# A state-space block and a routed expert layer: start, tail, router's choice and the table of stages rewritten

## The chip, the cores and the metric

One NeuronCore of a Trainium2 chip runs the whole program. Its engines work side by side and meet through semaphores: TensorE (PE), VectorE (DVE), ScalarE (ACT), GpSimd (POOL) and SyncE (SP), which issues most transfers (DMA). The metric is the device time of one execution in microseconds (us), lower is better. Three runs of the kernel before gave 2983.3, 2983.3 and 2991.5, median 2983.32. A difference of 0.3% or more (9 us) is counted as one.

## What is computed

Sixteen rows of 512 tokens by 256 features, all fp32. Two halves, each modulated by its own vectors (scale, shift, gate) made from a condition `c`:

```
mod = (silu(c) @ wmod).reshape(16, 6, 1, 256)          # sa, ca, ga, sb, cb, gb
h = layernorm(x) * (1 + ca) + sa
x = x + ga * mamba(h)                                  # norm, W_in, conv of 3, W_dt, scan over 512 steps
h = layernorm(x) * (1 + cb) + sb
x = x + gb * moe(h)                                    # 16 experts, all computed, weighted by the router
# scan: h = exp(dt * A) * h + (dt * x) * B ;  y = sum over 16 states of h * C
# router: scores = sigmoid(h @ gate.T); choice = scores + e_bias; 4 groups of 4 experts
#   group score = sum of its two best; keep 2 groups; in them the 4 best experts; weights normalised
```

The scan runs over 512 inner channels by 16 states. The experts are computed densely (every token through all 16) and combined with the router's weights, which are zero for those not chosen.

## The kernel before, in words

**Slots.** Each of the 16 rows has a slot of 32 units (`NU`). A unit is one state `n` of one pair of channel tiles: ScalarE makes the decays (`decay`, L981, two exponentials), GpSimd the drive (`drive`, L1120), VectorE scans 1024 elements (`scan`, L714) and multiplies by C (`times_c`, L721), and GpSimd adds the product to `gsum`, by its own adds for four units of sixteen and by an accumulating transfer (L1143) for the rest. SyncE broadcasts B and C rows from DRAM for each unit.

**The table.** A unit has 3 moments, a slot 96. All other work of the neighbouring rows is cut into steps and set beside the scan by the table in `streams`: an entry `(name, row, steps, first, final)` spreads the steps of a stage over the moments from first to final. The row before (`behind`) runs `mix1`, `project`, `stats` (second layernorm), `turn` (transposes, router logits), `pick` (router's choice, VectorE), `weigh` (weights transposed and stored); the row after (`coming`) runs `load_x`, `norms`, `turn_in`, `silu_first`/`silu_last` (convolution), `rows_bc`, `step_sizes0`; the slot's own row `gates`, `mix0`, `step_sizes1`. The experts of the row behind run from moment 35 of its slot to moment 22 of the next (`EXPERTS_AT`). Each engine has its own instruction order made by the same table, with a lag in moments: PE 0, ACT 1, DVE 2, POOL and SP 3. No engine reorders: what stands behind a waiting instruction waits too.

**Start.** SyncE issues all weights; then the modulation is computed and stored to DRAM; then 12 chunks of expert weights (512 KB each, three buffers in `gsum`) are loaded, transposed by PE through the three `wbank` buffers, and copied out half by ScalarE (L999), half by VectorE (L770); only then are the stages of row 0 done (`first_row`), and the first scan starts.

**Tail.** After the last scan the experts of row 14 finish over `TAIL` units, then `last_row` runs the stages of row 15 alone, then its 17 expert steps. A step is the gate and up products of one pair of experts on half the tokens (L461), tanh (L971), two products (L686, L693), the weighting (L1108) and the down product of the step before (L473).

**The choice.** `pick` has three parts (`yield` between them) and 22 waits and counts of its own semaphore, `ROUTE_V` = 26 per row.

## Time and profile before

| | us |
|---|---|
| median of three runs | 2983.32 |
| profiled execution | 2979.56 |
| its span, first to last instruction | 2977.7 |
| start, to the first scan | 131.31 |
| slot 0 | 140.09 |
| slot 1 | 164.68 |
| slots 2 to 14, each | 171 to 174 |
| slot 15 | 156.3 |
| tail, from the last scan's end | 147.9 |

VectorE is busy for 84% of the span, PE 81%, GpSimd 75%, ScalarE 53%; the mean granted clock of PE is 0.913. A slot is counted from its first scan to the next slot's. The idle time of an engine in front of an instruction stands in brackets with what released it, and a wait matters for the time only where the waiting engine is one that the others wait for.

### The profile page before, as it was taken

How to read it: one execution, taken by the hardware profiler on the slowest of the kernel's cores; microseconds unless marked ns; L12 is line 12 of the kernel's file. 1: busy time of each engine (PE TensorE's matmuls, PEld its weight loads, DVE VectorE, ACT ScalarE, POOL GpSimd, SP SyncE). 2: the span in 40 equal slices, each digit the busy share in tenths (PEclk: the TensorE clock that was granted, in tenths of full speed). 3: DMA queues.
4: the chain of work that ended last, by engine and by line, in shares of the span. 5: the costliest groups of instructions: out<-in, count | busy, mean ns of one | idle time of the engine just before them, and what ended most of it. 6: DMA issues, size and time to landing. Idle time of an engine off the chain costs nothing.

```text
span 2977.7 us, 29259 instructions
## 1 busy us (share of the span) xinstructions
PE 2415.1 (81%) x9004; PEld 1705.8 (57%) x9004; DVE 2495.4 (84%) x2673; ACT 1574.1 (53%) x2945; POOL 2234.5 (75%) x1514
## 2 busy tenths in 40 slices
PE   3525697988979798888979898897979889797879
PEld 2212465666746566665656566565656657565668
DVE  1389898989889898998989899898989889898932
ACT  2556555555556555555655555565565556554311
POOL 0388887878887787887878788787877878887912
PEclk8767898989989898998999899898999999898989
DMA  5188887787888777888887788788877878887921
GB/s 155 51 217 215 217 211 194 207 220 194 216 216 224 194 201 209 208 210 213 223 205 199 208 206 209 205 215 217 204 204 197 212 198 219 217 206 193 241 56 50
DMA packets 337374, 584.76 MB, mean 196 GB/s; under 512 B 50224, under 2 KB 153136, under 8 KB 337216
## 3 DMA queue, kind: packets, MB, share of 16 engines
q1 hardware_dynamic: 281920, 381.54, 41.1%
q0 software_dynamic: 55296, 201.35, 35.1%
q8 instruction: 71, 1.16, 0.2%
q14 instruction: 87, 0.71, 0.1%
HBM read 371.38 MB, written 10.06 MB: 128 GB/s over the span
## 4 chain that ended last, share of the span: by engine, by line
PE 39%; POOL 23%; issue 12%; DMA 10%; DVE 9%; ACT 6%; SPq 1%; POOLq 0%; DVEq 0%; ACTq 0%
PE wbank L461 12%; DMA gsum<-unit 9%; POOL unit L1120 9%; PE mbank L473 6%; POOL gsum L1143 4%; PE wbank L379 4%; DVE hbank L714 4%; PE wbank L417 3%; PE wbank L489 3%; POOL act L1108 3%; PE wbank L367 2%; PE wbank L437 2%; PE wbank L403 2%; POOL rstd L1043 2%; DVE unit L721 1%
## 5 line engine op out<-in xcount | busy, mean ns | idle before, releaser
L1120 POOL TENSOR_TENSOR unit<-dtx,b_bc 128x1024 f32<-128x1024 f32 x512 | 1310.5, 2578 | 11.0 <-DMA b_bc<-bc_scratch 9.2
L714 DVE TENSOR_TENSOR_SCAN hbank<-hbank,unit 128x1024 f32<-128x1024 f32 x512 | 1172.8, 2291 | 26.2 <-ACT hbank L981 20.9
L981 ACT ACTIVATE hbank<-dt,a_neg 128x512 f32<-128x512 f32 x1024 | 668.8, 680 | 319.6 <-DVE unit L721 316.8
L721 DVE TENSOR_TENSOR unit<-hbank,c_bc 128x1024 f32<-128x1024 f32 x512 | 624.1, 1219 | 28.8 <-DVE hbank L714 0.9
L1108 POOL TENSOR_TENSOR act<-act,w_all 128x512 f32<-128x512 f32 x256 | 356.8, 1394 | 299.0 <-DVE act L693 298.6
L473 PE MATMUL mbank<-down_t,act 128*128 128x256 f32 x2048 | 501.8, 382 | 55.1 <-POOL act L1108 52.3
L461 PE MATMUL wbank<-h_t,up_t 128*128 128x256 f32 x2048 | 490.0, 382 | 38.9 <-DVE xb L560 24.9
L461 PE MATMUL wbank<-h_t,gate_t 128*128 128x256 f32 x2048 | 502.9, 390 | 21.7 <-DVE act L686 14.4
L1143 POOL DMA_DIRECT2D gsum<-unit x384 | 366.2, 954 | 150.4 <-DVE unit L721 92.9
L473 PEld LDWEIGHTS mbank<-down_t,act 128*128 128x128 f32 x2048 | 382.8, 190 | 156.9 <-POOL act L1108 74.9
L461 PEld LDWEIGHTS wbank<-h_t,gate_t 128*128 128x128 f32 x2048 | 397.0, 196 | 125.8 <-DVE act L686 27.9
L461 PEld LDWEIGHTS wbank<-h_t,up_t 128*128 128x128 f32 x2048 | 384.9, 190 | 136.4 <-DVE xb L560 42.1
L971 ACT ACTIVATE etanh<-wbank 128x512 f32<-128x512 f32 x256 | 151.0, 590 | 401.2 <-PE wbank L461 401.2
L686 DVE SCALAR_TENSOR_TENSOR act<-etanh,wbank 128x512 f32<-128x512 f32 x256 | 173.9, 679 | 127.4 <-ACT etanh L971 127.3
L379 PE MATMUL wbank<-xb,w_dt 128*128 128x512 f32 x512 | 231.4, 596 | 8.6 <-DVE xb L560 8.4
L403 PE MATMUL wbank<-xn_t,w_in 128*128 128x512 f32 x256 | 182.1, 864 | 66.8 <-DVE gz L577 56.6
L351 PE MATMUL wbank<-ident,z 128*128 128x128 f32 x256 | 52.2, 359 | 173.5 <-ACT z L822 173.5
L693 DVE TENSOR_TENSOR act<-act,wbank 128x512 f32<-128x512 f32 x256 | 173.8, 679 | 18.5 <-PE wbank L461 13.6
L489 PE MATMUL wbank<-gsum,ident 128*128 128x512 f32 x256 | 130.3, 621 | 65.9 <-DMA gsum<-unit 65.9
L1037 POOL TENSOR_SCALAR nmean<-sums 128x4 f32<-128x4 f32 x48 | 20.5, 427 | 193.3 <-ACT ht L809 173.0
L379 PEld LDWEIGHTS wbank<-xb,w_dt 128*128 128x128 f32 x512 | 97.6, 191 | 110.5 <-issue 106.5
L1136 POOL TENSOR_TENSOR gsum<-unit 128x1024 f32<-128x1024 f32 x64 | 155.2, 2424 | 1.4 <-DVE unit L721 1.4
(124 smaller groups left out, 2534.0 us busy)
## 6 DMA issues: line engine op xcount, KB each, us to landing
gsum<-unit POOLq DMA_DIRECT2D x384, 512.0 KB, 7.5
b_bc<-bc_scratch SPq DMA_DIRECT2D x512, 256.0 KB, 6.4
c_bc<-bc_scratch SPq DMA_DIRECT2D x512, 256.0 KB, 5.7
w_all<-w_scratch SPq DMA_DIRECT2D x256, 256.0 KB, 4.4
ht<-in_L_attn_x_dram SPq DMA_DIRECT2D x16, 512.0 KB, 9.2
xt<-in_L_attn_x_dram SPq DMA_DIRECT2D x16, 512.0 KB, 9.0
out_dram<-xt SPq DMA_DIRECT2D x16, 512.0 KB, 3.3
z<-mod_scratch SPq DMA_DIRECT2D x16, 256.0 KB, 8.6
```

Source lines behind the costliest of these rows:

```text
L379: m = eng.matmul(t.bank[:, :], w_dt[:, k, m_ * P:(m_ + 1) * P], xb[:, xb_at(row, k), :], start=k == 0, stop=k == DK - 1)
L403: m = eng.matmul(t.bank[:, :], w_in[:, k, (DK + q) * P:(DK + q + 1) * P], xn_t[:, k, :], start=k == 0, stop=k == HK - 1)
L461: m = eng.matmul(t.bank[:, j * HT:(j + 1) * HT], w[:, 2 * first + j, k, :], h2_t[:, row % 2, k, h * HT:(h + 1) * HT], start=k == 0, stop=k ...
L473: m = eng.matmul(mbank[:, u * H:(u + 1) * H], act[:, (n - 1) % MOE_RING, j, u * P:(u + 1) * P], down_t[:, e, :], start=(e == 0 and u == 0) ...
L489: m = eng.matmul(t.bank[:, :], ident[:, :], gsum[:, (2 * p + k) % SUMS, a, :], start=False, stop=k == 1)
L686: eng.scalar_tensor_tensor(out=a, in0=etanh[:, :], scalar=1.0, in1=t.bank[:, :], op0=ALU.add, op1=ALU.mult).then_inc(t.free, 1)
L714: eng.tensor_tensor_scan(h, h, unit[:, g % RING, :, :].rearrange("p a t -> p (a t)"), 0.0, ALU.mult, ALU.add).then_inc(scanned, 1)
L721: eng.tensor_tensor(unit[:, g % RING, :, :], hbank[g % HB][:, :, :], c_bc[:, s:s + 1, :].to_broadcast([P, 2, T]), ALU.mult).then_inc(c_sca ...
L981: eng.activation(hbank[g % HB][:, a, :], dt[:, 2 * q + a, :], ACT.Exp, scale=a_neg[:, 2 * q + a, n:n + 1]).then_inc(decayed, 1)
L1108: eng.tensor_tensor(a, a, w_all[:, n % W_RING, :, :], ALU.mult).then_inc(weighted, 1)
L1120: eng.tensor_tensor(unit[:, g % RING, :, :], dtx[:, 2 * q:2 * q + 2, :], b_bc[:, s:s + 1, :].to_broadcast([P, 2, T]), ALU.mult).then_inc(d ...
L1143: eng.dma_start(o, unit[:, g % RING, :, :], accum_op=ALU.add).then_inc(summed[k], 16)
```

## The change

Four parts.

*Start.* SyncE loads what the modulation needs first, then row 0 of x, then the other weights and three chunks. ScalarE does the first layernorm of row 0 ahead of everything else, then the modulation. Only 4 of the 12 chunks (`EARLY`) are turned before the first scan; the other 8 are turned in slot 0, at moments 4 to 40. Their buffers are now both halves of `xt` and `act`.

*Choice.* `pick` computes a group's score as the greatest sum of two of its members, counts better groups with a small negative margin in place of greater-or-equal-and-earlier, and fuses scaling, masks and weights into `scalar_tensor_tensor` operations; `ROUTE_V` becomes 16.

*Table.* Many entries are moved by some moments, `gates` from 24..42 to 29..35 and `weigh` from 28..34 to 33..35 the most; `load_res` and `load_gb` come later; the lag of SP becomes 2.

*Tail.* `last_streams` sets the stages of row 15 among the last experts of row 14. Row 15's experts follow.

ScalarE at the program's start, before (then after). L986/L1006 is the exponential of `A_log`, L987/L998 and L993/L1004 the modulation, L999/L989 the copies of turned chunks, L809, L817, L822 (L808, L816, L821) sums, squares and scaling of a layernorm:

```order
L986 ACT_TABLE_LOAD
L986 ACTIVATE a_neg<-a_neg 128x64
L987 ACTIVATE dtx<-dtx 128x32
L993 ACTIVATE gz<-dt 16x256 x2
L999 ACTIVATE gate_t<-wbank 128x512
...
L999 ACTIVATE down_t<-wbank 128x512
L809 ACTIVATE ht,sums<-ht 128x256 x4
L817 ACTIVATE z,squares<-ht,nmean 128x256 x4
L822 ACTIVATE ht<-ht,shift,rstd 128x256 x4
L809 ACTIVATE ht,sums<-ht 128x256 x4
```

```order
L808 ACT_TABLE_LOAD
L808 ACTIVATE ht,sums<-ht 128x256 x4
L816 ACTIVATE z,squares<-ht,nmean 128x256 x4
L821 ACTIVATE ht<-ht,shift,rstd 128x256 x4
L998 ACTIVATE dtx<-dtx 128x32
L1004 ACTIVATE gz<-dt 16x256 x2
L1006 ACTIVATE a_neg<-a_neg 128x64
L989 ACTIVATE gate_t<-wbank 128x512
L989 ACTIVATE up_t<-wbank 128x512
L989 ACTIVATE down_t<-wbank 128x512
L989 ACTIVATE gate_t<-wbank 128x512
L808 ACTIVATE ht,sums<-ht 128x256 x4
```

The first layernorm stands ahead of the modulation now, and four copies are left between them and the second layernorm, where twelve were.

PE in slot 1, between the transposes of the second layernorm (L351, L352) and the first experts (L461, L476), before (then after). `w_in` are the gates of the slot's row, `w_tok` the router's weights:

```order
L351 MATMUL wbank<-ident,z 128x128 x8
L437 MATMUL wbank<-router_t,h_t 128x16 x8
L403 MATMUL wbank<-xn_t,w_in 128x512 x4
L351 MATMUL wbank<-ident,w_tok 16x128 x4
L403 MATMUL wbank<-xn_t,w_in 128x512 x2
L461 MATMUL wbank<-h_t,gate_t 128x256 x4
L461 MATMUL wbank<-h_t,up_t 128x256 x4
L403 MATMUL wbank<-xn_t,w_in 128x512 x2
```

```order
L352 MATMUL wbank<-ident,z 128x128 x8
L438 MATMUL wbank<-router_t,h_t 128x16 x8
L404 MATMUL wbank<-xn_t,w_in 128x512 x6
L352 MATMUL wbank<-ident,w_tok 16x128 x4
L404 MATMUL wbank<-xn_t,w_in 128x512 x2
L476 MATMUL wbank<-h_t,gate_t 128x256 x4
L476 MATMUL wbank<-h_t,up_t 128x256 x4
```

Three of four gates now stand ahead of the weights, the fourth right behind them, and all ahead of the experts.

PE in the tail, before: the last experts of row 14 (L461, L473), then `mix1` (L486, L489), `project` (L417, L419), `turn`, `weigh`, and row 15's first expert:

```order
L461 MATMUL wbank<-h_t,gate_t 128x256 x4
L461 MATMUL wbank<-h_t,up_t 128x256 x4
L473 MATMUL mbank<-down_t,act 128x256 x8
L486 MATMUL wbank<-xb,diag_d 128x512
L489 MATMUL wbank<-gsum,ident 128x512 x2
L486 MATMUL wbank<-xb,diag_d 128x512
L489 MATMUL wbank<-gsum,ident 128x512 x2
L417 MATMUL wbank<-w_out,gz 128x256 x4
...
L351 MATMUL wbank<-ident,z 128x128 x8
L437 MATMUL wbank<-router_t,h_t 128x16 x8
L351 MATMUL wbank<-ident,w_tok 16x128 x4
L461 MATMUL wbank<-h_t,gate_t 128x256 x4
```

The same place after, in two pieces, up to the first expert of row 15:

```order
L476 MATMUL wbank<-h_t,up_t 128x256 x4
L501 MATMUL wbank<-xb,diag_d 128x512
L504 MATMUL wbank<-gsum,ident 128x512 x2
L501 MATMUL wbank<-xb,diag_d 128x512
L504 MATMUL wbank<-gsum,ident 128x512 x2
L488 MATMUL mbank<-down_t,act 128x256 x2
L418 MATMUL wbank<-w_out,gz 128x256 x4
```

```order
L488 MATMUL mbank<-down_t,act 128x256 x2
L476 MATMUL wbank<-h_t,gate_t 128x256 x4
L476 MATMUL wbank<-h_t,up_t 128x256 x4
L488 MATMUL mbank<-down_t,act 128x256 x2
L352 MATMUL wbank<-ident,z 128x128 x8
L488 MATMUL mbank<-down_t,act 128x256 x2
L438 MATMUL wbank<-router_t,h_t 128x16 x8
L476 MATMUL wbank<-h_t,gate_t 128x256 x4
L476 MATMUL wbank<-h_t,up_t 128x256 x4
L488 MATMUL mbank<-down_t,act 128x256 x2
L352 MATMUL wbank<-ident,w_tok 16x128 x4
L488 MATMUL mbank<-down_t,act 128x256 x6
```

Two expert steps of row 14 now stand between `project` and the weights. The diff, cut to its core:

```diff
     EXPERTS_AT = (35, 118)
     EP = E // 2
+    LAST_EXPERTS_AT = (31, 122)
     HALVES = 4 * (E + 1)
-    ACT_LAG, DVE_LAG, POOL_LAG, SP_LAG = 1, 2, 3, 3
+    EARLY = 4
+    ACT_LAG, DVE_LAG, POOL_LAG, SP_LAG = 1, 2, 3, 2
     TAIL = 9
...
             behind, coming = slot - 1, slot + 1
-            plan = []
+            plan = [] if slot else [("chunks", 0, 2 * (len(chunks) - EARLY), 4, 40)]
             if behind >= 0:
-                plan += [("mix1", behind, 4, 6, 7), ("load_res", behind, 1, 1, 2), ("load_gb", behind, 1, 6, 30),
+                plan += [("mix1", behind, 4, 6, 7), ("load_res", behind, 1, 11, 11), ("load_gb", behind, 1, 57, 61),
                          ("project", behind, 4, 16, 16), ("stats", behind, 5, 19, 21),
-                         ("turn", behind, 4, 24, 25), ("pick", behind, 5, 26, 28), ("weigh", behind, 2, 28, 34)]
-            plan += [("step_sizes1", slot, 9, 1, 7), ("load_ga", slot, 1, 53, 60), ("gates", slot, 9, 24, 42),
-                     ("mix0", slot, 4, 51, 64)]
+                         ("turn", behind, 4, 24, 24), ("pick", behind, 5, 26, 28), ("weigh", behind, 2, 33, 35)]
+            plan += [("step_sizes1", slot, 9, 1, 7), ("load_ga", slot, 1, 57, 59), ("gates", slot, 9, 29, 35),
+                     ("mix0", slot, 4, 51, 63)]
             if coming < NB:
-                plan += [("load_x", coming, 1, 20, 24), ("norms", coming, 12, 25, 39), ("turn_in", coming, 2, 42, 47),
-                         ("silu_first", coming, 6, 56, 59), ("silu_last", coming, 6, 63, 65),
-                         ("rows_bc", coming, 3, 77, 84),
+                plan += [("load_x", coming, 1, 19, 26), ("norms", coming, 12, 25, 39), ("turn_in", coming, 2, 44, 47),
+                         ("silu_first", coming, 6, 56, 59), ("silu_last", coming, 6, 61, 65),
+                         ("rows_bc", coming, 3, 78, 83),
                          ("step_sizes0", coming, 9, 73, 79)]
             return [Steps(stage[name](row), n, first, final) for name, row, n, first, final in plan if name in stage]
...
-                        pass
+        def last_streams(stage):
+
+            last = NB - 1
+            plan = [("load_res", last, 1, 9, 12), ("mix1", last, 4, 5, 5), ("project", last, 4, 7, 7),
+                    ("stats", last, 5, 5, 9), ("turn", last, 4, 11, 12), ("load_gb", last, 1, 23, 23),
+                    ("pick", last, 5, 11, 15), ("weigh", last, 2, 13, 20)]
+            return [Steps(stage[name](row), n, first, final) for name, row, n, first, final in plan if name in stage]
...
+                tanhs = t.bank[:, 0:TT * E].rearrange("p (t e) -> p t e", e=E)
+                bias = choice_bias[:, :].rearrange("p (a e) -> p a e", a=1).to_broadcast([P, TT, E])
                 need.wait_ge(route_act, row + 1)
-                eng.tensor_scalar(scores, scores, 0.5, 0.5, ALU.mult, ALU.add).then_inc(route_v, 1)
+                eng.scalar_tensor_tensor(out=r_ch[:, :, :], in0=tanhs, scalar=0.5, in1=bias, op0=ALU.mult,
+                                         op1=ALU.add).then_inc(route_v, 1)
+                eng.tensor_scalar(r_s[:, :, :], tanhs, 1.0, None, ALU.add).then_inc(t.free, 1)
+                members = r_ch[:, :, :].rearrange("p t (g m) -> p (t g) m", m=GRP)
                 need.wait_ge(route_v, at + 1)
-                eng.tensor_copy(r_s[:, :, :], scores).then_inc(route_v, 1)
-                eng.tensor_tensor(r_ch[:, :, :], scores, bias, ALU.add).then_inc(route_v, 1)
-                eng.tensor_tensor(scores, scores, bias, ALU.add).then_inc(route_v, 1)
-                choice = scores.rearrange("p t (g m) -> p t g m", m=GRP)
-                pairs = r_ch[:, :, :].rearrange("p t (g m) -> p (t g) m", m=GRP)
-                kept = r_ch[:, :, :].rearrange("p t (g m) -> p t g m", m=GRP)
-                hi, lo = (r[:, :, :].rearrange("p (t g) m -> p t g m", t=TT) for r in (r_hi, r_lo))
+                eng.tensor_tensor(r_two[:, :, 0:3], members[:, :, 0:3], members[:, :, 1:4], ALU.add).then_inc(route_v, 1)
+                eng.tensor_tensor(r_two[:, :, 3:5], members[:, :, 0:2], members[:, :, 2:4], ALU.add).then_inc(route_v, 1)
+                eng.tensor_tensor(r_two[:, :, 5:6], members[:, :, 0:1], members[:, :, 3:4], ALU.add).then_inc(route_v, 1)
                 need.wait_ge(route_v, at + 4)
...
+                eng.tensor_reduce(r_g[:, :], r_two[:, :, :], AX.X, ALU.max).then_inc(route_v, 1)
...
+                need.wait_ge(route_v, at + 5)
+                eng.tensor_tensor(r_gt[:, :, :, :], other, this, ALU.subtract).then_inc(route_v, 1)
+                need.wait_ge(route_v, at + 6)
+                eng.tensor_tensor(r_gt[:, :, :, :], r_gt[:, :, :, :], low, ALU.is_gt).then_inc(route_v, 1)
+                need.wait_ge(route_v, at + 7)
...
+                need.wait_ge(route_v, at + 8)
+                eng.scalar_tensor_tensor(
+                    out=r_tmp[:, :, 0:E].rearrange("p t (g m) -> p t g m", m=GRP),
+                    in0=r_cnt[:, :].rearrange("p (t g a) -> p t g a", t=TT, a=1).to_broadcast([P, TT, NGRP, GRP]),
+                    scalar=1.5, in1=members.rearrange("p (t g) m -> p t g m", t=TT), op0=ALU.is_lt,
+                    op1=ALU.mult).then_inc(route_v, 1)
+                yield
...
+                need.wait_ge(t.free, t.after)
+                need.wait_ge(route_v, at + 12)
+                eng.scalar_tensor_tensor(out=r_w[:, :, 0:E], in0=r_cut[:, :, 0:E], scalar=TAKEN, in1=r_s[:, :, :],
+                                         op0=ALU.is_equal, op1=ALU.mult).then_inc(route_v, 1)
+                need.wait_ge(route_v, at + 13)
                 eng.tensor_reduce(r_den[:, :], r_w[:, :, :], AX.X, ALU.add).then_inc(route_v, 1)
-                need.wait_ge(route_v, at + 22)
-                eng.tensor_scalar(r_den[:, :], r_den[:, :], 1e-20, 2.0, ALU.add, ALU.mult).then_inc(route_v, 1)
-                need.wait_ge(route_v, at + 23)
+                need.wait_ge(route_v, at + 14)
                 eng.reciprocal(r_rec[:, :], r_den[:, :]).then_inc(route_v, 1)
-                need.wait_ge(route_v, at + 24)
...
                     "p (t a) -> p t a", a=1).to_broadcast([P, TT, E]), ALU.mult).then_inc(route_v, 1)
-                assert at + 25 == ROUTE_V * (row + 1)
+                assert at + 16 == ROUTE_V * (row + 1)
...
+            first_norms = norms(0)
+            for _ in range(5):
+                next(first_norms)
+            need.wait_ge(mod_w_in, 16 * N_MOD_LOADS)
             eng.activation(c_th, c_t, ACT.Tanh, scale=0.5).then_inc(c_act, 1)
...
+                beside = streams(slot, stage_of) if run else last_streams(stage_of)
+                young = experts_of(slot - 1, experts) if run else Halves(
+                    experts(NB - 1), HALVES, *LAST_EXPERTS_AT)
...
+            for dst, src in SMALL_LOADS[:N_MOD_LOADS]:
+                eng.dma_start(dst, src).then_inc(mod_w_in, 16)
+            eng.dma_start(ht[:, 0, :, :], d["L0_attn_x"][0].rearrange("(t p) h -> p t h", p=P)).then_inc(x_in, 16)
+            for dst, src in SMALL_LOADS[N_MOD_LOADS:]:
+                eng.dma_start(dst, src).then_inc(weights_in, 16)
+            for n in range(3):
+                load_chunk(n)
+            need.wait_ge(mod_dve, 6)
+            eng.dma_start(mod_dram, modr[:, 0:NMOD * H]).then_inc(mod_out, 16)
+            turning = turn_chunks()
+            for _ in range(2 * EARLY):
+                next(turning)
             need.wait_ge(mod_out, 16)
 
             stage_of = {"load_x": load_x, "load_res": load_res, "load_ga": load_ga, "load_gb": load_gb, "rows_bc": rows_bc,
-                        "weigh": weigh}
```

## Rows read from the trace of the kernel before

**Rows 1.** Busy time by stage (--windows): start, slot 0, slot 5, slot 15, tail.
```profile
core 0: us, PE busy (x) PEld busy (x) DVE busy (x) ACT busy (x) POOL busy (x), PEclk, DMA share, GB/s
0.00:131.31 131.31, 59.37 (x176) 31.44 (x176) 24.68 (x47) 40.90 (x84) 13.84 (x24) 0.78 0.38 102
131.31:271.40 140.09, 49.59 (x90) 19.08 (x90) 124.25 (x87) 79.67 (x142) 116.87 (x73) 0.66 0.80 202
950.00:1122.56 172.56, 148.21 (x558) 105.23 (x557) 154.70 (x167) 97.64 (x183) 140.16 (x96) 0.94 0.80 208
2673.52:2829.80 156.28, 129.28 (x510) 98.15 (x509) 145.44 (x151) 68.82 (x118) 126.47 (x81) 0.93 0.85 219
2829.80:2977.70 147.90, 124.39 (x551) 105.39 (x549) 42.47 (x91) 19.54 (x43) 27.84 (x25) 0.91 0.19 53
```

**Rows 2.** Waits of VectorE in slots 1 to 15: total, times, longest.
```profile
DVE act L686 <- ACT etanh L971: 67.5, 59, 1.7
...
DVE gz L577 <- ACT gz L918: 31.3, 15, 2.2
DVE wbank L604 <- ACT wbank L952: 29.5, 15, 2.0
```

**Rows 3.** Timeline of the start: start, duration (us), engine, line, operation.
```profile
24.82 0.21 ACT L987 ACTIVATE dtx<-dtx 128x32 f32<-128x32 f32 x1
...
37.68 0.35 SPq L1293 DMA_DIRECT2D mod_scratch<-dt  x1
...
39.12 2.16 SPq L1301 DMA_DIRECT2D gsum<-in_L_ffn_down_proj_dram  x4
...
43.38 0.60 ACT L999 ACTIVATE gate_t<-wbank 128x512 f32<-128x512 f32 x1 [6.69 <-PE wbank L509]
...
47.65 0.69 DVE L770 COPY down_t<-wbank 128x512 f32<-128x512 f32 x1 [1.01 <-PE wbank L509]
...
66.67 0.42 ACT L809 ACTIVATE ht<-ht 128x256 f32<-128x256 f32 x1 [0.23 <-DMA ht<-in_L_attn_x_dram]
...
74.76 2.34 POOL L1059 TENSOR_TENSOR ht<-ht,z 128x1024 f32<-128x1024 f32 x1 [2.19 <-ACT ht L822]
...
131.31 2.30 DVE L714 TENSOR_TENSOR_SCAN hbank<-hbank,unit 128x1024 f32<-128x1024 f32 x1 [4.99 <-POOL unit L1120]
```

**Rows 4.** Transfers issued before 62 us, median us to landing (last number).
```profile
w_in<-in_L_attn_W_in_dram SPq DMA_DIRECT2D x1, 1024.0 KB, 8.6
```

**Rows 5.** Slot 0: transfers and their landing.
```profile
gsum<-unit POOLq DMA_DIRECT2D x23, 512.0 KB, 7.4
...
z<-mod_scratch SPq DMA_DIRECT2D x1, 256.0 KB, 9.8
```

**Rows 6.** Slot 0: a scan that waits for ScalarE (timeline).
```profile
172.54 2.30 DVE L714 TENSOR_TENSOR_SCAN hbank<-hbank,unit 128x1024 f32<-128x1024 f32 x1 [2.94 <-ACT hbank L981]
```

**Rows 7.** The router's choice of row 15 in the tail (timeline, VectorE).
```profile
2880.37 0.23 DVE L604 TENSOR_SCALAR wbank<-wbank 128x64 f32<-128x64 f32 x1 [14.83 <-ACT wbank L952]
...
2882.19 0.23 DVE L633 TENSOR_TENSOR r_gt<-r_g 128x64 f32<-128x64 f32 x1
...
2883.83 0.41 DVE L654 MAX8 r_m<-r_tmp 128x8 f32<-128x16 f32 x4
...
2885.13 0.23 DVE L663 TENSOR_TENSOR r_sel<-r_cut,r_tmp 128x64 f32<-128x64 f32 x1
...
2886.32 0.23 DVE L673 TENSOR_TENSOR w_tok<-r_w,r_rec 128x64 f32<-128x64 f32 x1
```

**Rows 8.** The tail: last add of the scan, then row 15's stages (timeline).
```profile
2831.45 0.85 POOL L1143 DMA_DIRECT2D gsum<-unit  x1 [1.66 <-DVE unit L721]
...
2849.88 1.88 PE L489 MATMUL wbank<-gsum,ident 128*128 128x512 f32 x4
...
2864.85 0.69 DVE L593 TENSOR_TENSOR xt<-wbank,xt 128x512 f32<-128x512 f32 x1
...
2887.50 3.62 PE L461 MATMUL wbank<-h_t,gate_t 128*128 128x256 f32 x8
...
2892.68 1.89 PE L461 MATMUL wbank<-h_t,gate_t 128*128 128x256 f32 x8
```

More of the change, by code:

```diff
@@ L1209, in load_res @@
                     need.wait_ge(row_out, 16 * (row - 1))
+                else:
+                    t = work.at["turned", len(chunks) - 1, 1]
+                    need.wait_ge(t.full, t.after)
                 eng.dma_start(xt[:, row % 2, :, :], d["L0_attn_x"][row].rearrange("(t p) h -> p t h", p=P)).then_inc(
@@ L1284, in experts, with load_chunk @@
                     yield
[L1287 to L1294 removed]
+            def load_chunk(n):
+                src, _, split = chunks[n]
                 if n >= 3:
```

254 lines of the change are left out of this document (118 added, 136 removed).

## The prediction

> **What bounds the kernel now.** I read the busy times by stage first [rows 1]. The time is a sum of stretches with different limits: the start of 131.3 us (PE 59 us busy, VectorE 25: nothing is full, a chain of dependent steps sets it), slot 0 of 140.1, fifteen slots that add up to 2829.8 - 271.4 = 2558.4, so 170.6 each, and the tail of 147.9. In slot 5 VectorE is busy 154.7 of 172.6 us, PE 148.2, GpSimd 140.2, and the DMA engines 80%. So VectorE paces the slots and two others stand close behind. Second, the waits of VectorE in slots 1 to 15 [rows 2]: 67.5 us for tanh of the experts, 31.3 us for a gate's tanh (15 times, so 2.1 us in every slot), 29.5 us for the logits' tanh. A us taken off VectorE, or off one of these waits, should shorten the slot unless PE, GpSimd or a transfer is then late. Third, the timelines of the start [rows 3] and of the tail [rows 8], where each step waits for the one before.
>
> **The start.** Before, ScalarE starts the modulation at 24.82 and its store is issued at 37.68: 12.9 us. The first chunk's copy is at 43.38, the layernorm starts at 66.67, and GpSimd's first product with the modulation is at 74.76: 8.1 us of layernorm [rows 3]. From 74.76 to the first scan at 131.31 are 56.5 us, in which neither the operations nor their order change; I keep them. What moves is the 74.76. After: x of row 0 is issued fourth, at some 3.8 us. The nearest row for a load in that crowd is w_in, 8.6 us to landing [rows 4]: 12.4. The layernorm takes 8.1: 20.5. The modulation's tanh is queued on ScalarE behind it and has its data by then: 12.9 more, 33.4. SyncE stores it, then waits for three chunks to be turned before it loads the modulation's row. Three chunks took 43.38 to 48.3 before [rows 3], 5 us, and the third wait is followed by 2.2 us of issuing: 40.6. That row lands in 4 us (my low value, the queue being short) to 9.8 [rows 5]: 44.6 to 50.4, I take 46.6. So the first scan comes 74.8 - 46.6 = 28 us earlier. Bounds: 22 (x lands late, the row takes 9.8) and 33 (both early). The copies of the fourth chunk stand on ScalarE ahead of the second layernorm, but they are over before GpSimd's two products are.
>
> **Slot 0.** It takes over eight chunks: per chunk one copy of 0.69 on VectorE [rows 3], 0.6 from start to start, 8 x 0.6 = 4.8 us, and eight copies of 0.6 on ScalarE. VectorE is busy 124 of 140 us here, so its copies count in full. ScalarE is only 57% busy, but VectorE already waits for its decays where the layernorm stands in front of them [rows 6], 2.94 us at once, and the gates are now packed into the same units: I add 2 us. Total +7. The lower bound is 0 (the copies fall into waits that are there anyway). The upper one comes from the transfers. Six chunks of 512 KB are now loaded beside the accumulating transfers, which take 7.4 us each [rows 5], and two bare units of scan and product are 2 x 3.5 = 7.0: the transfers are level with VectorE already. At the 202 GB/s of the slot [rows 1] a chunk is 2.6 us of all DMA engines, six are 15.6; if every one delays the chain of sums, slot 0 is 5 + 15.6, about 20 us longer.
>
> The Trainium skill (DMA: Bandwidth & Descriptors, Queues, rings and completion order) says that each DMA engine takes turns between the queues that have work, packet by packet. By it a chunk on SyncE's queue does slow the sums on GpSimd's queue, and slot 0 would cost nearer 20 than 7; the trace shows a share of 0.80 but no chunk beside a sum, so no row decides it.
>
> **The router's choice.** In the tail it runs alone: first part 2880.37 to 2882.19, second to 2883.83, maxima and replacement to 2885.13, end 2886.55 [rows 7]. That is 1.82 + 1.64 + 1.42 = 4.88 us without the untouched 1.3 in the middle, for 24 operations. In the same rows an operation that waits for the one before starts 0.25 us after it (1.64 / 7 = 0.23, 1.42 / 6 = 0.24). After there are 14: six in the first part (three wait, three at about 0.12: 1.1 us), four in the second (1.0), four in the last (1.0): 3.1. So 1.8 us less of VectorE per row. A three-way broadcast into an operation with two steps has no row; if the fused ones cost 0.1 more each, 1.5 is left.
>
> **The table.** Of the moved entries I price one. Before, VectorE's first gate product stands at moment 28 (26 + lag), between the first and second part of the choice, and waits 2.1 us in every slot for a tanh that waits for PE [rows 2]. After, it is at moment 31, behind the whole choice, while PE still does the gate right behind the logits. That wait goes, and PE's for the router's weights gets shorter, as the order shows the gates ahead of them. Of 1.8 + 2.1 = 3.9 us I keep 3.0 per slot: what is late next is the first expert (PE now needs three banks that the packed gates free at moments 31 to 36), and the accumulating transfers, which end before `mix0`. Bounds: 0 (all is given back there) and 5.0 (the expert's waits, 67.5 / 15 = 4.5 us a slot [rows 2], shrink by a quarter too). load_res, load_gb and load_ga land several units before their use; SP's lag of 2 puts its stage loads ahead by one moment, between the same B and C loads in most cases. Both at nothing. Fifteen slots: -45 us, bounds 0 and -75.
>
> **The tail.** Before, row 15's `mix1` comes after all of row 14 (its sums read from 2849.88), its x is done at 2864.85 + 0.69 = 2865.5, its first expert starts at 2887.5, 22 us later [rows 8]. After, PE meets `mix1` behind expert 13's products at about 2834.7 and then waits for the last sum: issued 2831.45, 7.4 to landing, 2839 to 2840. So x is done 10 to 11 us earlier, near 2854.7. In the 22 us to the first expert PE was mostly idle; two expert steps of row 14 now fill that, and delay it only by the last down products, 2.8 us (12 passes of 1.89 / 8), while the choice takes 1.8 off: 2854.7 + 22 + 2.8 - 1.8 = 2877.7, 10 earlier. Against: row 15's first weights are loaded only behind row 14's output and gb, which waits for the last down product; about 1 us. For: the first eight passes after the idle time took 3.62 us against 1.89 later [rows 8], at the lower clock. I take -10, bounds -5 and -14.
>
> The Trainium skill (TensorE: Matmul & The Clock Gate, Part 1) says that an idle PE is put on half its clock; the trace agrees (3.62 against 1.89), and by it the shorter gaps give back up to 1.7 us, which would make the term nearer -12.
>
> **Sum.** -28 + 7 - 45 - 10 = -76. On the profiled execution's 2979.6 that is 2903.6. The median of the runs is 3.7 us above it, so I give 2907.
>
> **Rivals.**
> - *The slots give nothing* (0.18). VectorE's gain turns into waits for PE or the sums. For: PE 148 and GpSimd 140 busy of 172, DMA 80%. Against: neither is full. Slots 0 to -1 us each: 2983.3 - 31 - 8 = 2944.
> - *The slots give more* (0.13): 5 us each, 2877.
> - *Chunks and sums collide*, the rule of the queues (0.06): slot 0 at +20 and half of the slots' gain lost to later sums: 2907 + 13 + 22 = 2942.
> - *Slower* (0.04). ScalarE is the place: four gates in six moments beside the layernorm of the next row put its decays behind them, as in slot 0, where one such wait is 2.94 us [rows 6]. Two a slot are 5.9, less the choice's 1.8: +4.1 x 15 = +62, with -31 from the ends 3014. It decides from 31 / 15 = 2.1 us a slot on. Against: in slots 1 to 15 ScalarE is busy only 57%.
> - That the modulation isn't really earlier, because ScalarE does the layernorm first, is in the start's own bound (22).
>
> **Chances.** Forecast 0.59, its own range 2887 to 2927. Range for 8 in 10: 2872 to 2946. About 0.3%, 9 us, is what can be told from no change: faster 0.94, within 0.02, slower 0.04.
>
> **What would show it.** First scan near 103 us, GpSimd's first product near 47; slot 0 at 147; slots 2 to 14 near 168.5, without a wait for the gate's tanh; row 15's first expert 48 us after the last scan's end, before 57.7. Wrong: slots at 171 or more, a wait for decays of 2 us or more in each, or gate tanh waits replaced by equal ones for experts.

## The result and the profile after

The changed kernel takes 2886.55 us (median of four runs, 2885.14 to 2895.14), the kernel before on the same chip 2986.43 (2983.3 to 2991.5): a ratio of 0.967, 95% interval 0.9644 to 0.9696. 2907 was predicted, with a range of 2872 to 2946; the forecast's own narrower range ended at 2887, and the median lies 0.5 below it. The profiled execution took 2885.27 us, its span is 2883.5; against the profiled execution of before that is -94.3, where the prediction's sum was -76.

Busy time by stage in the profile after, to set beside [rows 1]: start, slot 0, slot 5, slot 15, tail. The columns are the stretch, its length, busy us of PE, PE's weight loads, VectorE, ScalarE and GpSimd with their instructions, PE's granted clock, the DMA engines' share and GB/s:

```profile
0.00:95.71 95.71, 43.58 (x112) 18.14 (x112) 19.04 (x40) 35.90 (x76) 13.88 (x25) 0.84 0.40 108
95.71:247.47 151.76, 65.72 (x154) 30.38 (x154) 128.70 (x94) 83.68 (x150) 117.79 (x74) 0.66 0.81 208
907.85:1076.13 168.28, 147.68 (x558) 105.94 (x557) 152.99 (x157) 97.45 (x183) 139.35 (x94) 0.93 0.82 213
2588.83:2743.91 155.08, 128.85 (x502) 96.89 (x501) 144.56 (x141) 68.54 (x118) 126.71 (x81) 0.92 0.88 221
2743.91:2883.50 139.59, 126.59 (x559) 106.85 (x557) 40.63 (x81) 19.67 (x44) 27.79 (x25) 0.96 0.21 58
```

| stretch | before | after | difference | predicted |
|---|---|---|---|---|
| start | 131.31 | 95.71 | -35.6 | -28 (-22 to -33) |
| slot 0 | 140.09 | 151.76 | +11.7 | +7 (0 to +20) |
| slots 1 to 15 | 2558.4 | 2496.4 | -62.0 | -45 (0 to -75) |
| tail | 147.9 | 139.6 | -8.3 | -10 (-5 to -14) |

VectorE's waits in slots 1 to 15 (us in all, times, longest), to set beside [rows 2]. The wait for the gate's tanh (L586 now, L577 before) went from 31.3 to 7.2 us; the experts' tanh and the logits' tanh stayed:

```profile
DVE act L677 <- ACT etanh L970: 66.3, 62, 2.0
DVE r_ch L614 <- ACT wbank L951: 29.5, 15, 2.0
DVE hbank L705 <- ACT hbank L980: 15.7, 34, 1.3
DVE gz L586 <- ACT gz L917: 7.2, 15, 0.6
```

The start after (start us, us, engine, line, tiles, and in brackets the idle time before and its releaser), to set beside [rows 3]: sums of row 0's layernorm, tanh of the modulation, its store, the load of its row, GpSimd's first product with it:

```profile
11.32 0.42 ACT L808 ACTIVATE ht<-ht 128x256 f32<-128x256 f32 x1 [9.25 <-DMA ht<-in_L_attn_x_dram]
19.23 0.21 ACT L998 ACTIVATE dtx<-dtx 128x32 f32<-128x32 f32 x1
31.40 0.35 SPq L1328 DMA_DIRECT2D mod_scratch<-dt  x1
36.81 0.47 SPq L1214 DMA_DIRECT2D z<-mod_scratch  x1
40.34 2.34 POOL L1068 TENSOR_TENSOR ht<-ht,z 128x1024 f32<-128x1024 f32 x1 [23.12 <-DMA z<-mod_scratch]
```

The tail after, to set beside [rows 8]: the second layernorm's transposes, row 14's last gate product, row 15's first one, GpSimd's first weighting in row 15, and the down product that waits for it:

```profile
2775.05 1.06 PE L352 MATMUL wbank<-ident,z 128*128 128x128 f32 x8 [4.44 <-ACT z L821]
...
2780.85 3.76 PE L476 MATMUL wbank<-h_t,gate_t 128*128 128x256 f32 x8
...
2792.03 1.89 PE L476 MATMUL wbank<-h_t,gate_t 128*128 128x256 f32 x8
...
2800.51 2.49 POOL L1117 TENSOR_TENSOR act<-act,w_all 128x512 f32<-128x512 f32 x2 [10.36 <-DMA w_all<-w_scratch]
2801.82 1.99 PE L488 MATMUL mbank<-down_t,act 128*128 128x256 f32 x8 [2.72 <-POOL act L1117]
```

### The profile page after: what moved, and what is told of

It reads as the page before. It is cut to its first block, busy times and chain, and to the rows that moved or that the text cites. A ratio compares the mean times of both kernels' runs of the same rounds, so it can differ in the third digit from the quotient of the medians.

```text
span 2883.5 us, 29133 instructions
## 1 busy us (share of the span) xinstructions
PE 2415.4 (84%) x9004; PEld 1719.6 (60%) x9004; DVE 2467.0 (86%) x2514; ACT 1569.0 (54%) x2945; POOL 2232.1 (77%) x1515
## 4 chain that ended last, share of the span: by engine, by line
PE 38%; POOL 18%; DVE 16%; issue 13%; ACT 8%; DMA 6%; SPq 0%; POOLq 0%; DVEq 0%; ACTq 0%
PE wbank L476 12%; PE mbank L488 7%; DVE hbank L705 7%; POOL unit L1129 7%; PE wbank L380 4%; PE wbank L418 4%; DMA gsum<-unit 3%; DVE unit L712 3%; POOL gsum L1152 3%; PE wbank L504 3%; POOL act L1117 3%; DMA ht<-in_L_attn_x_dram 2%; PE wbank L368 2%; ACT hbank L980 1%; PE wbank L438 1%
## 5 line engine op out<-in xcount | busy, mean ns | idle before, releaser
L705 DVE TENSOR_TENSOR_SCAN hbank<-hbank,unit 128x1024 f32<-128x1024 f32 x512 | 1172.9, 2291 | 36.8 <-ACT hbank L980 31.4
L712 DVE TENSOR_TENSOR unit<-hbank,c_bc 128x1024 f32<-128x1024 f32 x512 | 624.1, 1219 | 26.5 <-DMA c_bc<-bc_scratch 0.5
L488 PE MATMUL mbank<-down_t,act 128*128 128x256 f32 x2048 | 516.8, 392 | 67.2 <-POOL act L1117 67.2
L476 PE MATMUL wbank<-h_t,gate_t 128*128 128x256 f32 x2048 | 504.5, 390 | 9.8 <-DVE xb L569 9.6
L488 PEld LDWEIGHTS mbank<-down_t,act 128*128 128x128 f32 x2048 | 395.3, 195 | 167.6 <-POOL act L1117 83.3
L476 PE MATMUL wbank<-h_t,up_t 128*128 128x256 f32 x2048 | 486.0, 380 | 1.1 <-DVE act L677 0.6
L476 PEld LDWEIGHTS wbank<-h_t,gate_t 128*128 128x128 f32 x2048 | 400.4, 197 | 110.5 <-issue 33.7
L476 PEld LDWEIGHTS wbank<-h_t,up_t 128*128 128x128 f32 x2048 | 388.3, 190 | 81.3 <-issue 13.4
L404 PE MATMUL wbank<-xn_t,w_in 128*128 128x512 f32 x256 | 176.2, 850 | 44.0 <-DVE gz L586 31.9
L352 PE MATMUL wbank<-ident,z 128*128 128x128 f32 x256 | 51.7, 356 | 168.8 <-ACT z L821 150.6
L352 PEld LDWEIGHTS wbank<-ident,z 128*128 128x128 f32 x256 | 40.4, 184 | 182.4 <-issue 143.9
```

The lines of the kernel that those rows point to most:

```text
L404: m = eng.matmul(t.bank[:, :], w_in[:, k, (DK + q) * P:(DK + q + 1) * P], xn_t[:, k, :], start=k == 0, stop=k == HK - 1)
L476: m = eng.matmul(t.bank[:, j * HT:(j + 1) * HT], w[:, 2 * first + j, k, :], h2_t[:, row % 2, k, h * HT:(h + 1) * HT], start=k == 0, stop=k ...
L488: m = eng.matmul(mbank[:, u * H:(u + 1) * H], act[:, (n - 1) % MOE_RING, j, u * P:(u + 1) * P], down_t[:, e, :], start=(e == 0 and u == 0) ...
L705: eng.tensor_tensor_scan(h, h, unit[:, g % RING, :, :].rearrange("p a t -> p (a t)"), 0.0, ALU.mult, ALU.add).then_inc(scanned, 1)
L712: eng.tensor_tensor(unit[:, g % RING, :, :], hbank[g % HB][:, :, :], c_bc[:, s:s + 1, :].to_broadcast([P, 2, T]), ALU.mult).then_inc(c_sca ...
```

## The experiments

All start from the changed kernel. What a change does is read from the stretches of the profiled executions. The ratios to the kernel before have intervals of about 0.0015 either way (4.5 us), the changed kernel's own of 0.0026 (8 us), so a difference of a few us doesn't show in them. "Slots" below are slots 1 to 15 in the profile, 2496.4 in the changed kernel; "per slot" is the mean of slots 2 to 14, 167.84 there and 172.11 before. How far a slot's sum can be trusted is in the last section: the same slots, in kernels that differ elsewhere, gave 2491.2 to 2503.1.

### The router's choice as it was

```diff
-    ROUTE_V = 16
+    ROUTE_V = 26
 ...
-                eng.tensor_tensor(r_gt[:, :, :, :], other, this, ALU.subtract).then_inc(route_v, 1)
+                eng.tensor_tensor(r_gt[:, :, :, :], other, this, ALU.is_gt).then_inc(route_v, 1)
+                eng.tensor_tensor(r_eq[:, :, :, :], other, this, ALU.is_equal).then_inc(route_v, 1)
```

> The changed kernel with the router's choice as it was (24 operations instead of 14), all else kept. Theory (VectorE paces the slots): each removed us of VectorE shows in full, so slots 1 to 15 lose 15 x 1.8 = 27 us, the tail 1.8 more: about 29 slower than the changed kernel, 2914 on its profiled 2885. Rival (the slots are paced by what stands behind VectorE, and the gain came from the table): less than 10 slower, below 2895. If the fused operations are dearer than thought, 15 to 24.

2906.76 us median, ratio 0.9719 (0.9706 to 0.9732), where the changed kernel has 0.967. Slots 2514.1, so +17.7, and 168.93 per slot. VectorE is 1.6 us a slot busier (2008.24 over 13 slots against 1987.24), where 1.8 was forecast, and 1.1 of it shows. That lies in the weaker class of the expectation (15 to 24), but not for its reason: the fused operations aren't dearer, each takes 0.23 us. The 1.8 us that the tail was to lose aren't seen: it is 138.6 here, 139.6 in the changed kernel.

### The gates and the weights at their old moments

```diff
-("weigh", behind, 2, 33, 35)
+("weigh", behind, 2, 28, 34)
-("gates", slot, 9, 29, 35)
+("gates", slot, 9, 24, 42)
```

> The changed kernel with only two entries of the table as they were: gates at 24 to 42 and the weights at 28 to 34. Theory of the prediction: VectorE's first gate product stands between two parts of the choice again and waits 2.1 us for the gate's tanh in each slot (31 us in all), so 15 x 2 = about 30 us slower than the changed kernel, 2915, and that wait is back. Rival (the slots' gain of the table comes from the loads, not from the gates): under 8 slower, even with the wait back, since another wait shrinks.

2918.99 us, ratio 0.9755 (0.9742 to 0.9769). Slots 2528.4, +32.0, and 170.05 per slot. VectorE's waits in slots 1 to 15 of this kernel:

```profile
DVE act L677 <- ACT etanh L970: 63.5, 55, 1.8
DVE gz L586 <- ACT gz L917: 41.8, 15, 3.0
```

The wait for the gate's tanh is back, and larger than the 31.3 us of before: 41.8 - 7.2 = 34.6 us more waiting, 32.0 us more time. A wait of VectorE inside a slot was worth its length here. The two entries were moved together, so which of them makes the wait isn't told apart.

### The three loads at their old moments

```diff
-("load_res", behind, 1, 11, 11), ("load_gb", behind, 1, 57, 61), ("load_ga", slot, 1, 57, 59)
+("load_res", behind, 1, 1, 2),   ("load_gb", behind, 1, 6, 30),  ("load_ga", slot, 1, 53, 60)
```

> The changed kernel with only three loads at their old moments: the residual at 1 to 2, gb at 6 to 30, ga at 53 to 60. The prediction held these moves worth nothing: within 4 us of the changed kernel, 2881 to 2889. Rival: the residual's load of 512 KB at moment 1 runs beside the last sums that mix1 waits for at moment 6 (PE waited 56.5 us for these sums before, 27.5 after); by that 29 us of PE's waiting return, and if VectorE feels them 15 to 29 slower, 2900 to 2914.

2890.59 us, ratio 0.966 (0.9643 to 0.9676). Slots 2493.2, so -3.2, within what such sums swing. Moving the loads is worth nothing, and PE's waits for the sums are not from them: 29.4 us here, 27.5 in the changed kernel.

### The whole old table

> The changed kernel with the whole table of the slots and the lag of SyncE as they were; the choice, the start, the chunks in slot 0 and the tail are the new ones. Of the 62 us that slots 1 to 15 gained, the choice keeps about 27, so 35 us slower than the changed kernel: 2920. If the table is worth only the gates' wait: 30. If gains of choice and table can't be added, since both lie in the same wait: 50 or more. If the choice gives nothing by itself: 62.

2937.64 us, ratio 0.9813 (0.9799 to 0.9827). Slots 2546.8, +50.4, and 171.32 per slot: the case in which the gains of choice and table can't be added. The new choice keeps 11.6 us of the 62.0 (0.8 per slot) under the old table, and 17.7 under the new one. VectorE's waits show where the rest of its 1.6 us goes:

```profile
DVE act L677 <- ACT etanh L970: 70.4, 58, 1.8
DVE gz L586 <- ACT gz L917: 43.0, 15, 3.0
...
DVE xb L569 <- PE wbank L504: 11.4, 14, 1.1
```

The first gate product stands behind part of the choice and waits for a tanh that comes when it comes. A quicker choice only makes VectorE arrive earlier: 43.0 us of waiting instead of 31.3, which is 0.8 of the 1.6 us per slot.

### Five more entries as they were

```diff
-("turn", behind, 4, 24, 24), ("mix0", slot, 4, 51, 63), ("turn_in", coming, 2, 44, 47)
+("turn", behind, 4, 24, 25), ("mix0", slot, 4, 51, 64), ("turn_in", coming, 2, 42, 47)
-("silu_last", coming, 6, 61, 65), ("rows_bc", coming, 3, 78, 83)
+("silu_last", coming, 6, 63, 65), ("rows_bc", coming, 3, 77, 84)
```

> The changed kernel with five other entries of the table as they were: the second transposes' end 25, mix0 to 64, turn_in from 42, silu_last from 63, rows_bc 77 to 84. The whole old table cost 50.4 us in slots 1 to 15 (2546.8 against 2496.4 in their profiles), the gates' two entries alone 32.0, the three loads nothing (-3.2). Theory: the 18 us left lie in these entries, since with the old table PE waits 58.5 us for the last sums ahead of mix0 and mix1 (32.3 with only the gates old) and VectorE 11.4 us for PE's mix in the convolution (4.8): slots 2511 to 2518. Rival: they come from SyncE's lag of 3 or from x's load, or from the entries together only: 2493 to 2503 here.

2894.78 us, ratio 0.9677 (0.9662 to 0.9691). Slots 2502.4, +6.0, in the range of the rival and within what such sums swing. Of the table's 50.4 us, 32.0 are the gates and weights, -3.2 the loads, 6.0 these five; the other 15.6 come from SyncE's lag with x's load, or only from the entries together. VectorE's waits for PE's mixes (L569 and L719) point the same way: 16.4 us before, 15.8 with the whole old table, and 3.4 to 6.1 with any one group of entries as it was (4.5 in the changed kernel). Which it is stays open: the lag was not tried alone.

### All chunks before the first scan

```diff
-    EARLY = 4
+    EARLY = 12
```

> The changed kernel with all 12 chunks turned before the first scan, the new order of the start otherwise kept. Slot 0 should fall from 151.8 to about 140 to 142 if the chunks alone made it longer, and the start grow. Theory: the modulation is stored before the chunks, but its row is loaded only behind them on SyncE, and eight more chunks are about 22 us there (12 chunks took 43.38 to 66.67 before), so the first scan comes at 95.7 + 20 = 116 and the whole is about 8 to 12 us slower than the changed kernel. Rival: the chunks cost as much in slot 0 as at the start, no difference (within 4).

2892.91 us, ratio 0.9679 (0.9664 to 0.9694). The start and slot 0 of this kernel:

```profile
0.00:108.78 108.78, 56.09 (x176) 27.76 (x176) 24.57 (x49) 40.67 (x84) 13.89 (x25) 0.84 0.46 124
108.78:251.40 142.62, 49.51 (x90) 18.99 (x90) 124.15 (x87) 79.61 (x142) 118.25 (x74) 0.65 0.79 200
```

Eight chunks at the start cost 13.1 us, not 20: the row's load is issued at 48.71 there, 11.9 later than in the changed kernel, since the turning begins before the modulation is stored. In slot 0 they cost 9.1. So moving them is worth 4 us, which is what the rival said (within 4) and not the theory's 8 to 12, and the other 22.5 us of the start's 35.6 come from the new order alone. Most of the 9.1 isn't the chunks' own: the next experiment takes 7.0 of it away with the chunks still in slot 0.

### x of row 1 loaded first in slot 0

```diff
-("load_x", coming, 1, 19, 26)
+("load_x", coming, 1, 19, 26) if slot else ("load_x", coming, 1, 1, 1)
```

> The changed kernel, but in slot 0 SyncE loads x of row 1 at moment 1, ahead of the chunks from the eighth on, instead of at 19 to 26. Theory: VectorE's one wait of 9.7 us for decays in slot 0 comes from ScalarE, which waits 11.1 us for this load; with it early the wait goes and slot 0 falls from 151.8 to 143 to 145, so 7 to 9 us faster, 2877. Rival: the length of slot 0 is made by the transfers and copies of the chunks, the wait is only where it shows: slot 0 stays within 3 us of 151.8, and another wait takes its place.

2883.45 us, ratio 0.9638 (0.9623 to 0.9654), against the changed kernel's 0.967; the intervals overlap, and the profiled executions are equal (2885.05 and 2885.27). What decides is slot 0, first the waits of ScalarE and VectorE there in the changed kernel:

```profile
ACT ht L808 <- DMA ht<-in_L_attn_x_dram: 11.1, 1, 11.1
...
DVE hbank L705 <- ACT hbank L980: 15.7, 7, 9.7
```

and then the slot in this one:

```profile
96.10:240.90 144.80, 64.85 (x154) 29.99 (x154) 128.66 (x94) 83.56 (x150) 117.31 (x74) 0.65 0.82 213
```

151.8 to 144.8: -7.0, with the same busy times and the same chunks. VectorE waits 5.6 us for decays instead of 15.7 (and 3.9 more for gates). So 7.0 of slot 0's +11.7 were one transfer of row 1's x, issued behind the chunks' transfers: it landed 14.8 us after its issue, where it took 7.8 in the kernel before. How the other 4.7 divide between the copies, of which VectorE alone does 4.5 us, and the packed gates isn't shown. With the gates at their old moments the slot took 149.5, but five kernels whose slot 0 is that of the changed one took 149.8 to 152.5, and the last kernel below, with the slot of this one, took 142.0.

### The tail as it was

```diff
-                beside = streams(slot, stage_of) if run else last_streams(stage_of)
+                beside = streams(slot, stage_of) if run else []
 ...
+            last_row(stage_of)
+            experts_of(NB - 1, experts).rest()
```

> The changed kernel with the tail as it was: row 15's stages alone, behind all of row 14's experts. Tail 147.9 before, of which the choice takes 1.8: 146; it is 139.6 in the changed kernel, so 6 to 7 us slower, 2891 to 2892. Rival: the low clock of PE in the new tail and its wait for the weights give back all, less than 3 slower.

2896.04 us, ratio 0.9685 (0.9671 to 0.9699). By the profile its tail is 150.8 us, 11.2 longer than the changed one, where 6 to 7 were expected. PE in it, around the last scan's end at 2742.33:

```profile
2738.68 3.78 PE L494 MATMUL mbank<-down_t,act 128*128 128x256 f32 x8 [3.21 <-POOL act L1123]
2742.26 3.05 PE L482 MATMUL wbank<-h_t,gate_t 128*128 128x256 f32 x8
2745.14 1.89 PE L482 MATMUL wbank<-h_t,up_t 128*128 128x256 f32 x8
```

PE entered it behind, at the low clock: eight passes in 3.78 and 3.05 us instead of 1.89. The profile counts that lag to the tail. In the profiles of the changed kernel and of the one before PE came in at the full clock (1.99 and 1.89 us). A kernel with the new tail that came in as slowly as this one is that with x loaded first:

```profile
2735.85 3.78 PE L488 MATMUL mbank<-down_t,act 128*128 128x256 f32 x8 [3.30 <-POOL act L1117]
2739.43 3.06 PE L476 MATMUL wbank<-h_t,gate_t 128*128 128x256 f32 x8
```

Its tail is 143.3, 7.5 shorter than 150.8: like compared with like, the new tail gives about what was expected. The intervals of the two ratios (0.9685 and 0.967) overlap and don't settle it.

### Row 15's weights loaded first

```diff
                 eng.dma_start(w_dram[row], rows_out[0:E, :]).then_inc(w_stored, 16)
+                if row == NB - 1:
+                    load_w(row, 0)
+                    load_w(row, 1)
```

> The changed kernel, but SyncE issues the first two loads of row 15's router weights right behind the store of them, ahead of row 14's output and the gb row. Theory: GpSimd waited 10.4 us and PE 2.7 us for the first of them in the tail; so 2 to 3 us faster, 2882 to 2883, tail 137. Rival: another wait (PE's tanh at the low clock) takes its place, within 1 us.

2885.93 us, ratio 0.964 (0.9625 to 0.9656). PE from row 15's first gate product on:

```profile
2800.03 1.89 PE L476 MATMUL wbank<-h_t,gate_t 128*128 128x256 f32 x8
2801.76 1.89 PE L476 MATMUL wbank<-h_t,up_t 128*128 128x256 f32 x8
2803.49 1.89 PE L476 MATMUL wbank<-h_t,gate_t 128*128 128x256 f32 x8
2805.21 1.89 PE L476 MATMUL wbank<-h_t,up_t 128*128 128x256 f32 x8
2806.94 1.89 PE L488 MATMUL mbank<-down_t,act 128*128 128x256 f32 x8
```

The down product follows at once, where it waited 2.72 us. From row 15's first gate product to the end it is 2888.5 - 2800.03 = 88.5 us, against 2883.5 - 2792.03 = 91.5: -3.0, as expected. In the ten kernels with the new tail and the old order of these loads that stretch took 91.5 or 91.6 six times and 93.2 or 93.3 four times, so the gain is no swing. The profiled execution as a whole is 5.0 us longer than the changed kernel's (2890.28), since its slots came to 2503.1; the gain is seen in its own stretch only.

### The choice one scan later

```diff
-("pick", behind, 5, 26, 28)
+("pick", behind, 5, 28, 29)
```

> The changed kernel with the router's choice at moments 28 to 29 instead of 26 to 28, so that on VectorE a scan stands ahead of it. VectorE waited 29.5 us (15 times 2.0) for the logits' tanh before and after the change. Theory (VectorE paces the slots, and a wait that is filled with the next scan is won in full, as the gates' was): slots 1 to 15 shorter by 25 to 30, 2468. Rival (PE and ScalarE behind it are late next: the first gate product, for whose bank PE already waits 2.2 us, comes a scan later): within 8 of 2496, or longer.

3007.22 us, ratio 1.0064 (1.005 to 1.0078): all of the gain and more is gone. Slots 2616.0, +119.6, 8.4 per slot. The theory fell, in two ways. First, VectorE around the choice in slot 5:

```profile
997.41 1.23 DVE L712 TENSOR_TENSOR unit<-hbank,c_bc 128x1024 f32<-128x1024 f32 x1
1003.52 2.30 DVE L705 TENSOR_TENSOR_SCAN hbank<-hbank,unit 128x1024 f32<-128x1024 f32 x1 [4.89 <-ACT hbank L980]
...
1007.48 2.02 DVE L638 SCALAR_TENSOR_TENSOR r_tmp<-r_cnt,r_ch 128x64 f32<-128x64 f32 x1
...
1011.91 2.42 DVE L657 SCALAR_TENSOR_TENSOR r_w<-r_cut,r_s 128x64 f32<-128x64 f32 x1
...
1014.83 1.90 DVE L664 TENSOR_TENSOR w_tok<-r_w,r_rec 128x64 f32<-128x64 f32 x1
```

The scan that was put ahead doesn't fill the wait. Its decays stand on ScalarE behind the logits' tanh, for which ScalarE itself waits 3.75 us, and behind half a layernorm: so the scan waits 4.89 us where the choice waited 1.97. Over the slots the waits for decays rose from 15.7 to 98.1 us, and the 29.5 us of waiting for the logits' tanh went. Second, three operations of 0.23 us take 2 us each. GpSimd at the same time:

```profile
1007.07 2.34 POOL L1129 TENSOR_TENSOR unit<-dtx,b_bc 128x1024 f32<-128x1024 f32 x1
...
1011.62 2.62 POOL L1068 TENSOR_TENSOR ht<-ht,z 128x1024 f32<-128x1024 f32 x1
1014.32 2.34 POOL L1070 TENSOR_TENSOR ht<-ht,z 128x1024 f32<-128x1024 f32 x1
```

Each of the three starts while a product of GpSimd runs and ends within 0.1 us of its end (1009.50 and 1009.41, 1014.33 and 1014.24, 1016.73 and 1016.66). Of the fifteen of each in slots 1 to 15, 14, 15 and 14 were held so, and they took 1.90, 2.42 and 1.79 us on the mean, against 0.23: +5.4 us a slot, and that is the larger share of the 8.4. The choice's old place was in a pause of GpSimd's.

### The late choice with half of the projection later

```diff
-("project", behind, 4, 16, 16),
+("project", behind, 4, 16, 16), ("project2", behind, 2, 17, 17),
```

> As with the late choice, and on VectorE alone the second half of the projection's products one moment later, behind the product by C: there it waits 33.0 us in all (14 times 2.4) for PE's last product, and 1.14 of each would be filled. Theory: 16 us more than the late choice alone, slots near 2452. Rival: the projection, layernorm, logits and choice are one chain, so a wait that is filled at its head comes back at the logits' tanh: no difference from the late choice alone (within 5).

Here `project2` is VectorE's second half of `project`. 3026.47 us, ratio 1.0126 (1.0109 to 1.0143), slots 2639.3: 23 us more than the late choice alone. Neither expectation holds: a wait filled at the head of the chain cost more than it gave. VectorE's wait for PE's last product fell from 33.0 to 17.1 us, as meant, but its waits for decays rose from 98.1 to 132.1. Why they grew so much wasn't settled.

### Both repairs

The diffs of x loaded first and of row 15's weights together.

> The changed kernel with the two repairs together: in slot 0 x of row 1 is loaded at moment 1, and in the tail SyncE issues row 15's first two weight loads right behind their store. Alone they took slot 0 from 151.8 to 144.8 (-7.0), and the stretch from row 15's first gate product to the end from 91.5 to 88.5 (-3.0). They lie in different stretches, so -10: 2875 on the changed kernel's profiled 2885, ratio to the kernel before near 0.9635. Rival: the slots between swing by some 5 us from run to run with PE's granted clock (slots 1 to 15 were 2493 to 2503 in kernels whose slots are the same), and the whole shows no gain over the changed kernel, ratio 0.966 to 0.967.

2876.28 us median (2866.36 to 2879.15, five runs), ratio to the kernel before 0.9613 (0.9598 to 0.9627), below the changed kernel's interval. Slot 0, slots 1 to 15, tail:

```profile
95.88:237.90 142.02, 63.30 (x154) 29.42 (x154) 128.83 (x94) 83.56 (x150) 117.32 (x74) 0.66 0.84 217
237.90:2729.11 2491.21, 2179.10 (x8174) 1559.85 (x8175) 2278.80 (x2301) 1429.82 (x2676) 2072.86 (x1393) 0.93 0.84 215
2729.11:2864.60 135.49, 124.33 (x565) 105.57 (x564) 40.75 (x81) 20.02 (x44) 27.80 (x25) 0.99 0.22 59
```

It is the fastest version here. Its profiled execution took 2866.36 us, 18.9 less than the changed kernel's, but it is the lowest of its five runs; the other four took 2873.07 to 2879.15. Of the 18.9, 9.7 are slot 0 and 3.0 the weights; the rest (slots -5.2, the tail's first part -1.1) is what swings. The two repairs had promised 10 and a ratio of 0.9635; the two stretches give 12.7.

## Why the prediction was right, and where its terms were off

The direction, the places and the mechanisms held, and 2886.55 lies in the range. It came out 20 us under the forecast: the gains of the start and of the slots were put too small, the cost of slot 0 too low, and the tail's gain 2 us too high.

**Start: -28 predicted, -35.6 measured, outside its own bound of -33.** The step was right: GpSimd's first product with the modulation moved from 74.76 to 40.34, and 55.4 us followed it, against the 56.5 that were kept. It was forecast for 46.6. The 6.3 us between are: x landed and the layernorm was done 1.3 earlier (19.23 for 20.5), the modulation took 12.2 from there instead of 12.9, SyncE was at the row's load 5.4 us after the store and not 7.2, and the row came 3.5 us after its issue. The last is the failed sizing: 6.0 was taken, between 4 and the 9.8 read in slot 0 [rows 5]. The nearest row wasn't read: the same transfer in the start of the kernel before, issued at 62.99 behind chunks as here, landed in 4.2 us (transfers of 60 to 76 us, the last number):

```profile
z<-mod_scratch SPq DMA_DIRECT2D x1, 256.0 KB, 4.2
```

The mean share of a stage is no guide to such a figure. Read over the transfer's own time, the share was 0.77 for the 3.5 us of the changed kernel (in a start of 0.40), 0.89 for these 4.2, and 1.05 for the 9.8 (in a slot of 0.80; the profile's share can read over 1 in a short stretch). What makes 9.8 of it was not tried.

**Slot 0: +7 predicted, +11.7 measured.** With row 1's x out of the way the chunks and the packed gates together cost 4.7 or less, under the 7. What was missed is the 7.0 us of row 1's x. The prediction looked for the chunks' damage in the accumulating transfers, on GpSimd's queue. It fell on an ordinary load, issued behind the chunks by the same engine, for which ScalarE waited 11.1 us, and behind which VectorE's decays stood: 9.7 us at once. The place named in [rows 6] was right (a layernorm ahead of decays), its releaser wasn't.

The rival of the Trainium skill (DMA: Bandwidth & Descriptors, Queues, rings and completion order: the engines take turns between queues, packet by packet) would have made slot 0 some 20 us longer. It didn't come. The 23 accumulating transfers of the slot landed in 7.2 us (median) beside the chunks and in 7.4 without them, and with x first, the six chunks still loaded beside the sums, the slot is 4.7 longer in all. What fell is the price of 2.6 us for every chunk; how the engines took turns, no run here shows.

**Slots: -45 predicted, -62.0 measured.** 3.9 us a slot had been found (1.8 from the choice, 2.1 from the gate's wait) and 0.9 held back for what is late next. The experiments give 2.1 for the gates and weights (32.0 / 15) and 1.2 for the choice (17.7 / 15); 0.8 is left for the other entries of the table. So the discount was right for the choice, where a third of the saved 1.6 went into other waits, and wrong for the wait, which came in full. (It didn't go to nothing, though: 7.2 of the 31.3 us are left.) The experts' tanh, from which the upper bound was made, stayed at 66.3 of 67.5. And the two aren't independent: a quicker choice lengthens the wait that the table removes. Under the old table it is worth only 0.8 a slot; neither part can be priced alone. Of the moves costed at nothing, the loads are nothing (-3.2), the five entries can't be told from it (+6.0), and 15.6 us belong to no group tried alone. This is the part of the term that was missed and not only mis-sized.

**Tail: -10 predicted, -8.3 measured.** Row 15's first expert starts 48.1 us after the last scan, as said (48). x is done 12.7 earlier in that count, 2 more than thought, but PE comes to row 14's last gate and up products at the low clock (3.76 and 2.81 us for 1.89). The Trainium skill's rule on an idle PE (TensorE: Matmul & The Clock Gate, Part 1) was to make the term nearer -12; the new tail has its own idle stretch, 4.44 us before the second layernorm's transposes, and the low clock behind it, so nothing was given back. The wait for the weights, put at about 1 us, was 2.72 for PE; removing it gave 3.0. The -8.3 compares two profiles in which PE entered the tail at the full clock. In eight others with the same tail it came in at the low one (the first eight passes in 3.2 to 3.8 us), and the tail was 140.9 to 143.3. So a tail also depends on the clock with which PE enters it.

**The slower rival** (decays behind packed gates, two waits of 2.94 a slot): VectorE waits 15.7 us for decays in fifteen slots, 1.0 each, none over 1.3. It didn't happen; ScalarE is busy for 58% of slot 5. Why the waits stay short was not tested.

## What to carry to other kernels

A wait of the pacing engine that one late step causes can be worth its full length, but only if what is put in its place doesn't itself hang on the same late engine: look at what stands in front of the filler's inputs on their own queue before moving it. A saved operation ahead of such a wait is lost in it, so find the wait first and price the two together. A transfer's landing time is to be read at the place it will run in, from the same transfer if the trace has it, and a bulk load is to be kept from standing ahead of the one small load that a chain waits for.
